# Edge sums over 32 nodes on four column groups, in batches of two chunks, and the edge half of the MLP's first layer done tile by tile among them

## Chip, cores and metric

The kernel runs on one core of one Trainium2 chip. The metric is the device time of one launch in microseconds; before the change it is 714.82 us, the median of 3 runs (714.66 to 717.14).

## What is computed

One block of a graph network. All 100,000 edges carry a row of 256 floats and a receiving node `dst`, sorted; `src` is not used in the arithmetic. There are 6,250 nodes, and the receivers are drawn as 6250 u^2, so low nodes have many edges (some 20 each around node 1,000) and high ones few (8 each at the end).

```python
aggr = jax.ops.segment_sum(edge_attr, dst, num_segments=6250)      # 102.4 MB of edges read once
collected = jnp.concatenate([layernorm(x), aggr], axis=-1)          # [6250, 512]
h = relu(collected @ W1 + b1); h = relu(h @ W2 + b2)                # 512->256->256
x = x + h @ W3 + b3
# then, on layernorm(x): slice attention with 8 heads x 64 slices
slice_weights = softmax((x_mid @ W_slice + b_slice) / temp)         # [6250, 8, 64]
# slice tokens, their attention, and the projection of slice_weights back to 256 columns, added to x
```

Everything is fp32.

## The kernel before

Three stages follow each other. The **edge stage** (to about 290 us) reads the edges in 98 chunks of 1,024 edges (1 MB) into a ring of four slots. Each chunk is eight subtiles of 128 edges. For a chunk VectorE builds one-hot matrices (`one_hot`, L752 to L757) that say for each edge which of WINDOW = 64 consecutive nodes it belongs to, counted from the lowest node of its group; TensorE multiplies them with the edge rows (`window_sums`, L1111 to L1128), which gives 64 nodes x 256 columns per group. Chunks 0 to 83 hold two groups of 512 edges, the others four groups of 256. Two groups run side by side in the array: 64 columns of weights each, and the results on the lower and the upper 64 partitions of one PSUM bank (`side_of`, L1118). ScalarE copies them to SBUF (`evacuate`, L635), TensorE turns them (`turn`, L1130), and VectorE adds each group's window into the table `agg` in SBUF at a column read from a register (L835 to L840); each add waits for the one before by `groups_added`. SyncE issues the edge loads (`chunk`, L377): a slot is loaded again once `win_psum` says that its sums are done. How a chunk's edges lie in a slot depends on the groups: chunks 0 to 39 are one stretch of eight edge rows (8 KB) per partition, 40 to 83 two of 4 KB, 84 on four of 2 KB.

Beside that, once per trip of four chunks, two tiles of x (128 nodes each) are loaded (L399), normalised (VectorE statistics L815 to L822, GpSimd L526 to L531, ScalarE L622), transposed (`ln_transposes`) and sent through the upper half of W1 (`first_layer_x`), so that `h1x` holds layernorm(x) @ W1a + b1 at the end of the stage.

The **MLP** (290 to 420 us) goes over tiles of 512 nodes, twelve full ones and a rest of 106: `layer1` multiplies `agg` by the lower half W1b, VectorE adds `h1x` (`add_h1`, L902), ScalarE applies relu (L662), `layer2`, relu (L665), `layer3`, VectorE adds to x and takes statistics (`residual`, L911 to L923), GpSimd adds b3 and computes the scale (L546, L517 to L519). The order on PE is written out by hand (L1251 to L1280): layer2(i), layer1(i+1), layer3(i). In between lie `fold_transposes`, the products that fold W_slice into W_x (L1264) and the biases (L1271).

The **attention part** follows, from the transpose at L1286 on: 49 tiles of softmax (L1293, L1310), the slice attention, and the projection of 49 tiles (L1382). The change leaves it as it is.

If some group's edges span more nodes than the window has, a flag is set (`far_flag`) and a branch computes all sums again by an exact, slow way; otherwise the branch is skipped.

Every fp32 matmul shows as two instructions in the trace; a transpose shows as one.

## Time and profile before

| | us |
|---|---|
| median of three runs | 714.82 |
| time of the profiled execution | 716.08 |
| its span | 714.3 |
| edge stage, to the last sum | 284.85 |
| MLP, from layer1(0) to the first transpose of the attention part | 290.24 to 419.28 |
| attention part | 419.28 to 714.3 |

```profile
span 714.3 us, 12349 instructions
PE 689.7 (97%) x3510; PEld 431.3 (60%) x3510; DVE 409.5 (57%) x985; ACT 305.1 (43%) x470; POOL 238.4 (33%) x308
...
PE   7899999999999999999999989999999999799997
...
DVE  6555545545555466453444378888888888522221
...
PEclk9999999999999999999999999999999999999999
DMA  8999999999999999200000004333333333212221
GB/s 314 393 375 408 393 406 408 407 405 404 407 404 404 394 384 313 75 1 0 0 0 0 0 1 60 73 70 62 73 71 62 72 73 66 38 59 73 81 81 65
...
PE 75%; DMA 20%; DVE 2%; issue 1%; SPq 1%; ACT 0%; DVEq 0%; ACTq 0%
```

The digit lines are the span in 40 slices of 17.9 us, each digit the busy share in tenths; the edge stage is the first 16 slices, where DMA is busy, the MLP the next seven. The last line is the chain of work that ended last, by engine.

### The profile page before, as it was taken

To read this page: it belongs to the slowest core of one execution; us is meant where nothing else is said; L and a number is where in the kernel's file an instruction comes from. 1 tells how busy PE (TensorE), PEld (TensorE's weight loads), DVE (VectorE), ACT (ScalarE), POOL (GpSimd) and SP (SyncE) were. 2 spreads that over 40 slices of the span, in tenths; PEclk is the share of its full clock that TensorE was granted. 3 is DMA by queue.
4 is the path that set the end of the run, shared out by engine and by line. 5 is a ranking of instruction groups with operands and counts; after the bars stand their busy time and mean duration, and the time that the engine had idled before them with its cause. 6 is when DMAs were issued, how large, how long until landed. Compare 5 with 4: busy or idle time off the path is not lost.

```text
span 714.3 us, 12349 instructions
## 1 busy us (share of the span) xinstructions
PE 689.7 (97%) x3510; PEld 431.3 (60%) x3510; DVE 409.5 (57%) x985; ACT 305.1 (43%) x470; POOL 238.4 (33%) x308
## 2 busy tenths in 40 slices
PE   7899999999999999999999989999999999799997
PEld 3666666666666666666556654444444444588886
DVE  6555545545555466453444378888888888522221
ACT  4233343333333434312221225545545545487773
POOL 3011011011010101313323336666666666254442
PEclk9999999999999999999999999999999999999999
DMA  8999999999999999200000004333333333212221
GB/s 314 393 375 408 393 406 408 407 405 404 407 404 404 394 384 313 75 1 0 0 0 0 0 1 60 73 70 62 73 71 62 72 73 66 38 59 73 81 81 65
DMA packets 95119, 131.72 MB, mean 184 GB/s; under 512 B 56825, under 2 KB 71117, under 8 KB 89983
## 3 DMA queue, kind: packets, MB, share of 16 engines
q1 hardware_dynamic: 94287, 131.26, 53.1%
q10 hardware_dynamic: 816, 0.26, 0.2%
q8 instruction: 8, 0.13, 0.1%
q14 instruction: 8, 0.07, 0.0%
HBM read 112.26 MB, written 6.40 MB: 166 GB/s over the span
## 4 chain that ended last, share of the span: by engine, by line
PE 75%; DMA 20%; DVE 2%; issue 1%; SPq 1%; ACT 0%; DVEq 0%; ACTq 0%
DMA ring_mem<-edge_attr_in 20%; PE ps L1124 14%; PE ps L1382 12%; PE ps L1293 12%; PE ps L1310 11%; PE ps L1246 6%; PE ps L1236 6%; PE ps L1228 6%; PE ps L1182 3%; PE ps L1286 2%; PE ps L1137 1%; PE ps L1174 1%; PE ps L1348 0%; DVE ring_mem L981 0%; DVE mx L983 0%
## 5 line engine op out<-in xcount | busy, mean ns | idle before, releaser
L1124 PE MATMUL ps<-ring_mem,side 128*64 128x256 f32 x1564 | 187.8, 386 | 8.1 <-DMA ring_mem<-edge_attr_in 6.0
L1124 PEld LDWEIGHTS ps<-ring_mem,side 128*64 128x64 f32 x1564 | 113.1, 137 | 68.8 <-issue 26.5
L756 DVE TENSOR_TENSOR side<-iota_w,rel 128x512 f32<-128x512 f32 x98 | 67.0, 686 | 94.2 <-PE ps L1137 94.1
L638 ACT ACTIVATE side<-ps 128x256 f32<-128x256 f32 (+1 forms) x98 | 40.7, 415 | 145.6 <-PE ps L1124 145.5
L1293 PE MATMUL ps<-ring_mem,xn 128*128 128x512 f32 x196 | 93.3, 599 | 0.9 <-DVE ring_mem L995 0.7
L1310 PE MATMUL ps<-side,ring_mem 128*128 128x512 f32 x196 | 92.3, 593 | 1.0 <-ACT ring_mem L674 1.0
L526 POOL TENSOR_TENSOR var_e<-mv,eps 128x2 f32<-128x2 f32 (+1 forms) x25 | 4.9, 195 | 237.8 <-DVE mv L822 237.8
L839 DVE TENSOR_TENSOR big<-big,ps 128x128 f32 x223 | 63.9, 287 | 30.1 <-issue 12.1
L1382 PE MATMUL ps<-side,ring_mem 128*128 128x256 f32 x360 | 77.9, 379 | 0.0
L584 POOL TENSOR_TENSOR ring_mem<-ring_mem 128x512 f32<-128x512 f32 x49 | 67.3, 1373 | 30.7 <-DVE ring_mem L995 30.1
L1382 PEld LDWEIGHTS ps<-side,ring_mem 128*128 128x128 f32 x360 | 68.4, 190 | 9.3
L689 ACT ACTIVATE ring_mem<-ring_mem 128x512 f32<-128x512 f32 x49 | 30.9, 630 | 89.5 <-POOL ring_mem L576 89.5
L735 ACT ACTIVATE ring_mem<-big 128x1024 uint16 (+1 forms) x45 | 60.7, 1358 | 15.6 <-PE ps L1382 15.6
L1310 PEld LDWEIGHTS ps<-side,ring_mem 128*128 128x128 f32 x196 | 36.9, 190 | 47.0 <-issue 45.0
L576 POOL TENSOR_TENSOR ring_mem<-ring_mem,mx 128x512 f32<-128x512 f32 x49 | 51.0, 1042 | 35.6 <-DVE mx L983 35.4
L1064 DVE TENSOR_TENSOR ring_mem<-ps,xn 128x256 f32<-128x256 f32 x49 | 20.8, 425 | 64.2 <-PE ps L1382 64.2
L602 POOL TENSOR_TENSOR xn<-x_sb,ring_mem 128x256 f32<-128x256 f32 x49 | 35.7, 732 | 55.7 <-DVE ring_mem L1064 43.2
L682 ACT ACTIVATE side<-ring_mem 128x1024 uint16<-128x1024 uint16 x49 | 51.8, 1058 | 1.0 <-DVE ring_mem L993 0.8
L1293 PEld LDWEIGHTS ps<-ring_mem,xn 128*128 128x128 f32 x196 | 33.4, 190 | 28.5 <-issue 26.0
L1182 PE MATMUL ps<-ln_t,w1a_sb 128*128 128x256 f32 (+1 forms) x200 | 48.9, 387 | 0.7 <-ACT ln_t L627 0.7
L1236 PE MATMUL ps<-ring_mem 128*128 128x512 f32 (+1 forms) x104 | 44.3, 569 | 0.8 <-ACT ring_mem L662 0.8
L1246 PE MATMUL ps<-ring_mem 128*128 128x256 f32 x196 | 44.5, 380 | 0.5 <-ACT ring_mem L665 0.5
(131 smaller groups left out, 820.1 us busy)
## 6 DMA issues: line engine op xcount, KB each, us to landing
ring_mem<-edge_attr_in SPq DMA_DIRECT2D x97, 1024.0 KB, 8.6
x_sb<-x_in SPq DMA_DIRECT2D x24, 256.0 KB, 7.0
result<-ring_mem SPq DMA_DIRECT2D x24, 256.0 KB, 2.1
big<-side SPq DMA_TRANSPOSE x49, 3.0
ring_mem<-edge_attr_in SPq DMA_DIRECT2D x1, 512.0 KB, 5.9
ring_mem<-L_gnn_W_in SPq DMA_DIRECT2D x2, 256.0 KB, 3.3
ring_mem<-L_ffn_W_x_in SPq DMA_DIRECT2D x2, 256.0 KB, 4.7
ring_mem<-L_ffn_W_fx_in SPq DMA_DIRECT2D x1, 512.0 KB, 3.7
```

Of the source, the lines that this page charges most:

```text
L584: pool.tensor_tensor(sw_sum, sw_sum, soft[:, (s - 1) % UNROLL, :], ALU.add).then_inc(sw_summed, 1)
L682: act.activation(halves[:, s % 2], words(soft[:, (s - 2) % UNROLL, :]), ACT.Copy).then_inc(split_ready, 1)
L735: act.activation(words(stage[:, s, :]), sw_t[:, bass.ds(t, 1)].rearrange("p t h n -> p (t h) n"), ACT.Copy).then_inc(staged, 1)
L756: dve.tensor_tensor(hot[:, b], iota_w[:, :].unsqueeze(1).broadcast_to(shape), where.unsqueeze(2).broadcast_to(shape), ALU.is_equal).then_i ...
L839: dve.tensor_tensor(win, win, pair[:, :, (g % 2) * WINDOW:(g % 2 + 1) * WINDOW], ALU.add).then_inc(groups_added, 1)
L1124: last = mm(ps[side_of * WINDOW:(side_of + 1) * WINDOW, SUM_BANKS[s % 2], pair * F:(pair + 1) * F], lhsT=hot[0:parts, s, t, :], rhs=ring8[ ...
L1182: last = mm(ps[:, bank, m * 256:m * 256 + n * P], lhsT=w1a_sb[:, k, m * P:(m + 1) * P], rhs=ln_t[:, k, 0:n * P], start=(k == 0), stop=(k = ...
L1236: last = mm(halves[m], lhsT=w2_sb[:, k, m * P:(m + 1) * P], rhs=h1_t[:, k, 0:cols], start=(k == 0), stop=(k == KF - 1))
L1246: last = mm(ps[:, 4 + a // 2, (a % 2) * F:(a % 2 + 1) * F], lhsT=h2_t[:, k, a * P:(a + 1) * P], rhs=w3_sb[:, k, :], start=(k == 0), stop=( ...
L1293: last = mm(ps[:, 4 + k, :], lhsT=xn[:, r, k * P:(k + 1) * P], rhs=soft[:, r, :], start=isinstance(t, int) and t == 3, stop=isinstance(t, ...
L1310: last = mm(ps[:, s % 2, :], lhsT=xn_t[:, s % 2, k, :], rhs=wc[:, k, :], start=(k == 0), stop=(k == KF - 1))
L1382: last = mm(ps[:, s, 0:F], lhsT=rows, rhs=m_blk[:, j, :], start=(j == 0), stop=(j == PAIRS - 1))
```

## The change

- **Groups and windows.** WINDOW is 32. A group is half as many edges: chunks 0 to 39 have two groups of 512, chunks 40 to 83 four of 256, and chunks 84 to 99 hold 896 edges on 112 partitions, four groups of 224. There are 100 chunks. Rows per partition are 4 KB for chunks 0 to 39 and 2 KB from 40 on.
- **Four column groups.** A group's sums take 32 columns of the array and 32 partitions of the result; four groups run side by side.
- **Batches.** PE, ACT and DVE go in batches of two chunks. With two groups per chunk, the four groups of a batch share one half of a bank, so that evacuation and turn are half as large; with four, each chunk's sums take one half. Window adds become 64 elements wide (two halves of 32) instead of 128; there are 319 instead of 223. `turn` uses two banks instead of four; banks 6 and 7 are for the new product.
- **x work.** Two tiles of x per batch instead of per trip, done by batch 27.
- **First layer for edges.** From trip 14 on, each trip of four chunks computes agg @ W1b for one tile of 512 nodes, one half per batch (`first_layer_edges`), and DVE adds it into `h1x` (`add_h1e`). Ahead of the first half PE waits until the adds of all earlier batches are done. Groups from there on take their window from no lower than the nodes already used. Eleven tiles are done so; tile 11 and the rest come after the stage.
- **MLP.** relu of the first layer reads `h1x` directly; layer2 uses two pairs of banks in turn; the order is layer2(i), layer3(i-1).
- **Loads.** W1b and W2 during the edge stage, W3 after chunk 97, b3 and W_x after the last sums, W_fx after the last third layer.

The diff, cut to its core:

```diff
-WINDOW = 64
+WINDOW = 32
+CHUNK_GROUPS = 4
 ROWS_PER_PART = 2
...
-TURN_BANKS = (2, 3, 6, 7)
+TURN_BANKS = (2, 3)
+H1E_BANKS = (6, 7)
...
+TWOS = 40
+FOURS = 84
+LAST_P = 112
+X_TRIPS = 13
+H1E_TRIP = 14
+H1E_TILES = 11
...
+def run_batches(eng, step):
+
+    def trip(i, groups, parts, what):
+        for h in range(2):
+            step(i * 2 + h, h, i, groups, parts, what)
+
+    trip(0, 2, P, "x")
+    trip(1, 2, P, "x")
+    with eng.Fori(2, TWOS // UNROLL) as i:
+        trip(i, 2, P, "x")
+    with eng.Fori(TWOS // UNROLL, X_TRIPS - 1) as i:
+        trip(i, 4, P, "x")
+    trip(X_TRIPS - 1, 4, P, "x")
+    trip(X_TRIPS, 4, P, "x")
+    with eng.Fori(H1E_TRIP, FOURS // UNROLL) as i:
+        trip(i, 4, P, "h1")
+    with eng.Fori(FOURS // UNROLL, H1E_TRIP + H1E_TILES - 1) as i:
+        trip(i, 4, LAST_P, "h1")
+    trip(H1E_TRIP + H1E_TILES - 1, 4, LAST_P, "h1")
 
 
...
+            def chunk_rows(c, groups, parts):
+                if parts == P:
+                    rows = edges[bass.ds(c * CHUNK_EDGES, CHUNK_EDGES), :]
+                else:
+                    rows = edges[bass.ds(c * LAST_EDGES + (E_LAST - FOURS * LAST_EDGES), LAST_EDGES), :]
+                return rows.rearrange("(g p k) f -> p g (k f)", g=groups, p=parts)
+
+            def slot(s, groups, parts):
+                return ring8[0:parts, s].rearrange("p (g k) f -> p g (k f)", g=groups)
...
+            def batch(b, h, i, groups, parts, what):
+                for j in range(2):
+                    c, s = b * 2 + j, h * 2 + j
+                    if past(c, UNROLL):
+                        sp.wait_ge(win_psum, c - (UNROLL - 1))
+                    if before(c, FULL_CHUNKS):
+                        sp.dma_start(slot(s, groups, parts), chunk_rows(c, groups, parts)).then_inc(edge_in[s], 16)
+                    else:
+                        tail_chunk(s, edge_in[s])
+                    if isinstance(c, int) and c == 0:
+                        rest_of_dst()
+                if isinstance(b, int) and b == 1:
...
+                if what == "x" and before(b, X_PAIRS):
+                    if past(b, 1):
+                        sp.wait_ge(x_in, b * 16)
+                    sp.dma_start(tiles_of(b * 2, 2),
+                                 x[bass.ds(b * (2 * P), 2 * P), :].rearrange("(t p) f -> p t f", p=P)
                                  ).then_inc(x_in, 16)
-
-            run_chunks(sp, chunk, 1, EDGE_TRIPS, CHUNKS, apart=True)
-
...
+                if isinstance(b, int) and b == X_PAIRS + 2:
+                    sp.dma_start(w1b_sb, w1[F:2 * F, :].rearrange("(k p) n -> p k n", p=P)).then_inc(w1b_in, 16)
+                    sp.dma_start(w2_sb, w2.rearrange("(k p) n -> p k n", p=P)).then_inc(w2_in, 16)
+            run_batches(sp, batch)
+            sp.wait_ge(win_psum, CHUNKS - 2)
+            sp.dma_start(w3_sb, w3.rearrange("(k p) n -> p k n", p=P)).then_inc(w3_in, 16)
+            sp.wait_ge(win_psum, CHUNKS)
+            sp.dma_start(b3_bc, b3.rearrange("(a n) -> a n", a=1).broadcast_to([P, F])).then_inc(b3_in, 16)
...
+            sp.wait_ge(l3_psum, MLP_CHUNKS + 1)
+            sp.dma_start(wfx_sb, w_fx.rearrange("(k p) n -> p k n", p=P)).then_inc(late_in, 16)
...
+            def relu_one(i, cols):
+                act.wait_ge(h1e_added, i * 2 + 3)
+                if past(i, 1):
+                    act.wait_ge(l2_psum, i)
+                act.activation(h1_t[:, :, 0:cols], h1x[:, :, bass.ds(i * 4 * P, cols)], ACT.Relu).then_inc(h1_ready, 1)
+
...
+            def relu_two(i, cols, halves):
                 act.wait_ge(l2_psum, i + 1)
+                if past(i, 1):
+                    act.wait_ge(l3_psum, i)
                 for m in range(KF):
                     act.activation(h2_t[:, m, 0:cols], halves[m], ACT.Relu,
                                    bias=b2_sb[:, m:m + 1]).then_inc(h2_ready, 1)
 
-            with act.Fori(0, MLP_CHUNKS) as i:
-                relus(i, 4 * P, [ps[:, 2 + m, :] for m in range(KF)])
...
+            relu_one(0, 4 * P)
+            for i in range(3):
+                relu_one(i + 1, 4 * P)
+                relu_two(i, 4 * P, l2_banks(i % 2))
...
+            with act.Fori(0, (MLP_CHUNKS - 4) // 2) as j:
+                for a in (1, 0):
+                    i = j * 2 + (4 - a)
+                    relu_one(i + 1, 4 * P)
+                    relu_two(i, 4 * P, l2_banks(a))
...
+                late = rel[:, TWOS:CHUNKS, :]
+                dve.wait_ge(prep_v, then(dve.tensor_scalar(below, late, 0.0, 8192.0, ALU.is_lt, ALU.mult)))
+                dve.wait_ge(prep_v, then(dve.tensor_tensor(late, late, below, ALU.add)))
...
+            def add_h1e(i, m, n=4, bank=None):
+                at = ps[:, H1E_BANKS[m], 0:n * P] if bank is None else ps[:, bank + m, 0:n * P]
+                cols = h1x[:, m, bass.ds(i * 4 * P, n * P)]
+                dve.wait_ge(h1e_psum, i * 2 + (m + 1))
+                dve.tensor_tensor(cols, cols, at, ALU.add).then_inc(h1e_added, 1)
...
+            def batch(b, h, i, groups, parts, what):
+                if before(b, BATCHES - 2):
+                    dve.wait_ge(win_psum, b * 2 + 2)
+                    for j in range(2):
+                        one_hot(b * 2 + (UNROLL + j), h * 2 + j)
+                if what == "h1":
+                    if h == 0:
+                        dve.wait_ge(h1x_ready, 2 * (X_PAIRS + 1))
+                    add_h1e(i - H1E_TRIP, h)
+                if h == 0:
+                    n_regs = UNROLL * groups
+                    dve.load(base_regs[0:n_regs], base_i[0:1, bass.ds(sums_ahead(b * 2, groups), n_regs)])
+                dve.wait_ge(sums_ready, b + 1)
+                turned_sums = ps[:, TURN_BANKS[h], :]
+                for j in range(2):
+                    c = b * 2 + j
+                    for g in range(groups if before(c, FULL_CHUNKS) else TAIL_GROUPS):
+                        dve.wait_ge(groups_added, sums_ahead(c, groups) + (CREDIT + g))
+                        win = agg[:, :, bass.ds(base_of[(h * 2 + j) * groups + g], WINDOW)]
+                        col, q = (0, j * 2 + g) if groups == 2 else (j * F, g)
+                        found = turned_sums[:, col:col + F].rearrange("p (k n) -> p k n", k=KF)
+                        dve.tensor_tensor(win, win, found[:, :, q * WINDOW:(q + 1) * WINDOW],
+                                          ALU.add).then_inc(groups_added, 1)
+                if what == "x" and before(b, X_PAIRS):
+                    dve.wait_ge(x_in, b * 16 + 16)
+                    for a in range(2):
+                        norm_stats(b, a)
+                    if past(b, 1):
+                        dve.wait_ge(rstd1_ready, b)
+                    norm_sums(b, 2)
...
+            for m in range(KF):
+                add_h1e(MLP_CHUNKS - 1, m)
+            for m in range(KF):
+                add_h1e(MLP_CHUNKS, m, n=1, bank=4)
...
+            def one_sum(b, h, j, g, t, q, col, parts, first, last):
+                return mm(ps[q * WINDOW:(q + 1) * WINDOW, SUM_BANKS[h], col:col + F],
+                          lhsT=hot[0:parts, h * 2 + j, t, :], rhs=ring8[0:parts, h * 2 + j, t, :], start=first, stop=last)
+
+            def window_sums(b, h, i, groups, parts):
+                pe.wait_ge(hot_ready, b * 2 + 2)
+                pe.wait_ge(edge_in[h * 2], i * 16 + 16)
+                if groups == 2:
+                    pe.wait_ge(edge_in[h * 2 + 1], i * 16 + 16)
+                    for n in range(per):
+                        for q in range(4):
+                            last = one_sum(b, h, q // 2, q % 2, (q % 2) * per + n, q, 0, parts, n == 0, n == per - 1)
+                    last.then_inc(win_psum, 2)
+                    return
+                for j in range(2):
+                    tail = not before(b * 2 + j, FULL_CHUNKS)
+                    if j == 1:
+                        pe.wait_ge(edge_in[h * 2 + 1], i * 16 + (32 if tail else 16))
+                    for n in range(per):
+                        for g in range(TAIL_GROUPS if tail else groups):
+                            rows = TAIL_PARTS if tail and g == TAIL_WHOLE else parts
+                            last = one_sum(b, h, j, g, g * per + n, g, j * F, rows, n == 0, n == per - 1)
+                    last.then_inc(win_psum, 1)
+
+            def turn(b, h, groups):
+                pe.wait_ge(win_ready, b + 1)
+                if past(b, 2):
+                    pe.wait_ge(groups_added, sums_ahead(b * 2 - 2, groups) + CREDIT)
+                for n in range(groups // 2 * KF):
+                    last = tr(ps[:, TURN_BANKS[h], n * P:(n + 1) * P], win_sb[:, h, n * P:(n + 1) * P], ident[:, :])
+            def first_layer_edges(i, m, n=4, bank=None):
+                to = ps[:, H1E_BANKS[m], 0:n * P] if bank is None else ps[:, bank + m, 0:n * P]
+                for k in range(KF):
+                    last = mm(to, lhsT=w1b_sb[:, k, m * P:(m + 1) * P], rhs=agg[:, k, bass.ds(i * 4 * P, n * P)],
+                              start=(k == 0), stop=(k == KF - 1))
+                return last
+
+            def batch(b, h, i, groups, parts, what):
+                window_sums(b, h, i, groups, parts)
+                if what == "x":
+                    if past(b, 3):
+                        first_layer_x(b - 3, 1 if isinstance(b, int) and b == X_PAIRS + 3 else 2)
+                    if past(b, 2) and before(b, X_PAIRS + 3):
+                        ln_transposes(b - 2, 1 if isinstance(b, int) and b == X_PAIRS + 2 else 2)
+                else:
+
+                    if h == 0:
+                        pe.wait_ge(w1b_in, 16)
+                        pe.wait_ge(h1x_ready, 2 * (X_PAIRS + 1))
+                        pe.wait_ge(groups_added, sums_ahead(b * 2, groups) + CREDIT)
+                    pe.wait_ge(h1e_added, (i - H1E_TRIP) * 2 + 1)
+                    first_layer_edges(i - H1E_TRIP, h).then_inc(h1e_psum, 1)
+                turn(b, h, groups)
...
+            pe.wait_ge(w2_in, 16)
+            pe.wait_ge(groups_added, sums_ahead(CHUNKS - 2, CHUNK_GROUPS) + CREDIT)
+            layer2(0, 4 * P, l2_banks(0))
+            pe.wait_ge(groups_added, CREDIT + ALL_SUMS)
+            pe.wait_ge(h1e_added, 2 * H1E_TILES + 1)
             for m in range(KF):
+                first_layer_edges(MLP_CHUNKS - 1, m).then_inc(h1e_psum, 1)
+            for m in range(KF):
+                first_layer_edges(MLP_CHUNKS, m, n=1, bank=4).then_inc(h1e_psum, 1)
+            layer2(1, 4 * P, l2_banks(1))
+            pe.wait_ge(w3_in, 16)
+            pe.wait_ge(h1e_added, 2 * (MLP_CHUNKS + 1) + 1)
             layer3(0, 4)
+            fold_transposes()
+            layer2(2, 4 * P, l2_banks(0))
             layer3(1, 4)
+            fold_weights()
+            layer2(3, 4 * P, l2_banks(1))
+            layer3(2, 4)
+            fold_biases()
+            with pe.Fori(0, (MLP_CHUNKS - 4) // 2) as j:
+                for a in (0, 1):
+                    i = j * 2 + (4 + a)
+                    layer2(i, 4 * P, l2_banks(a))
+                    layer3(i - 1, 4)
+            layer2(MLP_CHUNKS, P, [ps[:, 1, m * P:(m + 1) * P] for m in range(KF)])
             layer3(MLP_CHUNKS - 1, 4)
```

## Rows read from the trace of the kernel before

**Rows 1.** Busy time in stretches of the edge stage and of the MLP, PE to GB/s
```profile
0.00:20.00 20.00, 14.53 (x81) 7.83 (x81) 13.93 (x31) 9.25 (x5) 5.69 (x16) 1.00 0.85 313
60.00:120.00 60.00, 59.46 (x464) 40.34 (x466) 30.14 (x92) 22.77 (x51) 6.17 (x20) 1.00 1.01 403
180.00:240.00 60.00, 59.10 (x466) 40.09 (x464) 30.46 (x91) 22.63 (x50) 6.17 (x20) 1.00 1.03 405
246.00:270.00 24.00, 22.98 (x180) 16.08 (x178) 14.31 (x46) 9.80 (x18) 2.58 (x7) 1.00 1.05 384
303.00:415.00 112.00, 112.00 (x364) 67.27 (x362) 50.47 (x135) 24.78 (x33) 35.68 (x32) 1.00 0.00 0
```

**Rows 2.** Chain of waits in the edge stage; columns: start, length, what, instructions
```profile
231.71 8.74 DMA ring_mem<-edge_attr_in
254.31 10.53 DMA ring_mem<-edge_attr_in
269.71 3.60 PE ps L1124 x32
```

**Rows 3.** Timeline, edge stage, PE; columns: start, length, engine, line, what, idle before
```profile
182.46 0.66 PE L1174 MATMUL ps<-ident,xn 128*128 128x128 f32 x4
182.95 0.60 PE L1137 MATMUL ps<-ident,side 128*128 128x128 f32 x4
187.49 1.99 PE L1182 MATMUL ps<-ln_t,w1a_sb 128*128 128x256 f32 x8
259.55 1.95 PE L1124 MATMUL ps<-ring_mem,side 128*64 128x256 f32 x16 [0.75 <-DMA ring_mem<-edge_attr_in]
```

**Rows 4.** Groups of instructions; columns as in the page's part 5
```profile
L1124 PE MATMUL ps<-ring_mem,side 128*64 128x256 f32 x1564 | 187.8, 386 | 8.1 <-DMA ring_mem<-edge_attr_in 6.0
L1124 PEld LDWEIGHTS ps<-ring_mem,side 128*64 128x64 f32 x1564 | 113.1, 137 | 68.8 <-issue 26.5
L839 DVE TENSOR_TENSOR big<-big,ps 128x128 f32 x223 | 63.9, 287 | 30.1 <-issue 12.1
L981 DVE TENSOR_TENSOR ring_mem<-ps,side 128x512 f32<-128x512 f32 x49 | 33.9, 691 | 18.4 <-PE ps L1310 17.7
```

**Rows 5.** Timeline of DVE in the edge stage
```profile
185.30 0.43 DVE L815 BATCH_NORM_STATS2 bn<-x_sb 128x6 f32 x1
276.11 1.55 DVE L839 TENSOR_TENSOR big<-big,ps 128x128 f32 x4 [1.02 <-issue]
```

**Rows 6.** Timeline at the end of the edge stage, and line L388's landing
```profile
273.78 0.47 SPq L388 DMA_DIRECT2D ring_mem<-edge_attr_in  x1
...
DMA to landing us min/median/max: 7.3/7.3/7.3
...
281.18 3.67 PE L1124 MATMUL ps<-ring_mem,side 128*64 128x256 f32 x28
290.24 3.60 PE L1228 MATMUL ps<-big,side 128*128 128x512 f32 x8
```

**Rows 7.** Chain of waits in the MLP, one tile, then timeline at its end
```profile
342.12 3.43 PE ps L1228 x8
345.56 3.45 PE ps L1246 x16
349.01 3.43 PE ps L1236 x8
...
419.28 0.38 PE L1286 MATMUL ps<-ident,xn 128*128 128x128 f32 x2
```

**Rows 8.** Timeline of DVE, ACT and POOL beside one tile of the MLP
```profile
380.22 1.22 DVE L911 TENSOR_TENSOR x_sb<-x_sb,ps 128x1024 f32 x1 [2.29 <-PE ps L1246]
381.55 1.41 DVE L916 BATCH_NORM_STATS2 bn<-x_sb 128x6 f32 x4
383.44 1.27 ACT L665 ACTIVATE ring_mem<-ps,b_sb 128x512 f32<-128x512 f32 x2 [4.42 <-PE ps L1236]
384.86 2.35 POOL L546 TENSOR_TENSOR x_sb<-x_sb,ring_mem 128x1024 f32 x1
```

602 lines of the change are left out of this document (251 added, 351 removed).

## The prediction

> **What bounds the kernel now.** I read the stretches first. From 60 to 240 us, while edges are summed, the DMA engines are saturated at 403 to 405 GB/s, and PE is busy 59 of 60 us: two engines at their limit at once. From 246 on, where a chunk is stored in 2 KB rows instead of 4 KB, the rate is 384. From 303 to 415 no DMA runs and PE is busy all the time [rows 1]. The chain of waits says the same: it goes through landings of 8.74 us, and of 10.53 us where the rows are 2 KB [rows 2]. PE waits for the landing there, too (0.75 us at 259.55) [rows 3], so 384 is DMA's rate, not PE's. The MLP is one unbroken line of PE: three layers of 3.43 to 3.45 us per tile of 512 nodes [rows 7]. So a cut of PE's work in the edge stage alone gives nothing, as DMA stays; PE time made free there is worth something only if MLP work is moved into it. That is the change.
>
> **Sums on four column groups.** A chunk is 16 PE instructions (each fp32 matmul is two); two chunks together take 3.60 us [rows 2], 0.225 us per pair of instructions that run side by side on two column groups (one lasts 386 ns, 1564 of them fill 187.8 us [rows 4]). With four groups side by side the 32 instructions of a batch take 8 x 0.225 = 1.8 us; I take 2.0. Bounds: 1.8, and 3.6 if four are no better than two. The Trainium skill, TensorE: Matmul & The Clock Gate, Part 3, measured 2.38x for three column groups; that efficiency gives an estimate of 2.15 us, which hides as well.
> PE per batch in the x phase: 2.0 + 0.66 (four transposes of x) + 1.99 (first layer of x) + 0.3 (turn: two instructions for two chunks instead of four; 0.6 and four instead of eight where a chunk has four groups) [rows 3] = 5.0 us. DMA needs for it (1024 KB a chunk, 256 KB of x, by the page's list of issues) 2 x 1.049 MB + 0.262 MB of x at 405 GB/s = 5.82 us. DVE: two one-hots of 256 elements, each 0.42 (an operation takes 287 ns on 128 elements and 691 on 512, so 1.05 ns per element [rows 4]), four adds of 0.35 (below), 1.25 of x statistics (0.43 twice and three small steps [rows 5]), 0.3 of register loads: 4.0 us. DMA stays the bound, PE's cut is hidden, worth 0.
>
> **DMA of the edge stage.** Chunks 0 to 39 go from 8 KB rows (403) to 4 KB (405) [rows 1]: 0. Chunks 40 to 83 go from 4 KB to 2 KB: 44 x 1.049 MB x (1/384 - 1/405) = +6.2 us. Bound below: 0. By the Trainium skill, DMA: Bandwidth & Descriptors, Why small descriptors are slow, a packet carries about 3 fixed cycles beside one per 32 bytes; an estimate from that is 2.3%, 2.6 us instead of 6.2. I stay with the row.
> The w1b and w2 loads come into the stage: 0.52 MB at 384, +1.4. Before, the last chunk was issued at 273.78 and landed 7.3 us later, 281.1 [rows 6]; now 281.1 + 6.2 + 1.4 = 288.7. Batches release two slots at once; two others, 5.2 us of transfers, are then still queued, so DMA doesn't starve while sums end within that. At the start DVE gets two operations more on the index table (480 elements, some 0.65 each), PE waits for them ahead of the flag's transpose, and the next batch of sums is queued behind; the same queue of transfers covers it: 0, bound 3 us either way. The index table itself is one DMA more on SP, 0.4 us, ahead of the second chunk: in the same bound.
> Chunks 84 to 99 use 112 partitions. No row shows such a transfer. I take the rate of 384 (4 x 0.917 MB, 9.56 us per four chunks); the other end is that such a chunk takes as long as one on 128 partitions, 10.9 per four. That end speaks against the change, and the Trainium skill has a rule for it, SBUF — State Buffer, Door 1: a port serves eight partitions from separate stretches, and partitions 112 to 127 share their four ports with 80 to 95; a transfer without them leaves the other twelve ports as full as before, so by that rule 10.9.
>
> **First layer for edges inside the stage.** Each of 11 trips (four chunks) gets 3.44 us of PE [rows 7] and two DVE adds of 512 elements, 0.69 each [rows 4]. Sums, half a layer, turn: 2.0 + 1.72 + 0.6 = 4.3 us per batch against 4.8 to 5.46 of DMA. But there is a new wait: in each even batch PE waits until the previous batch's window adds are done; behind it stand its layer half, its turn and the next sums. DVE's adds also double in number (8 per batch). An add costs 0.42 from start to start (four in 1.55 [rows 5]), 0.13 of that beyond its 287 ns; at 64 elements 220 + 130 = 0.35, eight 2.8 us. 16 registers for the addresses cost 1.02 us [rows 5]. The loop per trip: PE half layer to its landing in DVE 2.1, add 0.69, registers 1.02, adds 2.8, two one-hots 0.83, add 0.69, adds 2.8 = 10.9 us. DMA wants 10.92 for the seven trips on 128 partitions (hidden) and 9.56 for the last four: +1.35 x 4 = +5.4 us. Bounds: 0 if DVE's steps overlap better, and if an add stays at 0.42, 12.0 us per trip: 7 x 1.1 + 4 x 2.45 = +17.4. Last sums end at 288.7 + 5.4 + 0.9 (one short chunk) = 295.0, where they end at 284.85 now [rows 6]: **+10.1**.
>
> **Tail and MLP.** Now 134.4 us pass from the end of the sums (284.85) to 419.28, where the attention part's first transpose starts [rows 6, 7]. Afterwards, in a row on PE: half layer 1.72, turn 0.55, twelve second layers 41.2, the small second layer 1.0 (moved ahead of that point), layer one of tile 11 and of the rest 4.4, twelve third layers 41.4, eight fold transposes 1.0, 24 instructions of fold products 3.1 (those on 128 columns at 0.13, from 0.60 for four [rows 3] less the drain): 94.4 us. **-40.0**. Eleven x 3.43 = 37.7 of it is the moved layer, the rest the x layer and transposes that stand now between 284.85 and 290.24 [rows 6]. Beside a tile of 6.9 us lie DVE 1.22 + 1.41 + 0.7 of small steps, ACT 1.27 and one more relu of that size, POOL 2.35 and some 1.4 of small steps [rows 8]: each under 4 us, their cover holds, and without it POOL would be next. The first second layer (3.43) covers the last seven window adds (2.5). The small second layer left its place after 419.28 (1.0), but DVE's last residual (3.4 us) ends last there: -0.2. The w_fx load waits for the last third layer, SP's transposes stand behind it; it costs 3.7 us of queue at most, with four tiles to go before a buffer comes back: 0. The w3, b3 and w_x loads land some 10 us before PE wants them: 0.
>
> **Sum**: +10.1 - 40.0 - 0.2 = -30.1. Profiled span 714.3 gives 684.2; that run's time was 716.08, 1.78 around the span; it lay 1.26 above the median 714.82. That gives **684.7**.
>
> **Rivals.**
> (a) The hand-over chain is longer: an add stays at 0.42 for the smaller window. For: the 0.13 between adds is waiting, not elements. Against: 512 and 128 elements do scale. 684.7 + 12 = 696.7. Chance 0.17.
> (b) DMA is kinder: 2 KB rows at 405 once PE is free, and DVE hides. Then 281.1 + 1.4 + 0.9 = 283.4: 684.7 - 11.6 = 673.1. Against: 384 held in a stretch where PE waited for DMA. 0.10.
> (c) Four groups no better than two: sums 3.6 per batch. x phase 6.6 against 5.82 in 20 batches and 6.8 against 6.14 in four: +17.5; edge trips 11.9 against 10.9: +11. 713. 0.06, no measurable change.
> (d) Slower than before: the weight loads of the narrow tiles don't overlap one another. A load lasts 137 ns, though now only 72 of it count (113.1 / 1564) [rows 4]. 32 x 0.137 = 4.4 us per batch: x phase 7.4 against 5.8 (+31 + 6 + 3), edge trips 13.5 against 10.9 (+28): 753. It decides from 3.7 us per batch, where the gain is gone. 0.05.
> (e) PE now idles 1 us or so in each batch, and the granted clock falls to 1.2 GHz: 4.3 becomes 8.6, 5.0 becomes 10, some +175 us. Against: it stayed at 1.00, that is 2.4 GHz, in the first 20 us too, with PE busy 14.5 of them [rows 1]. The Trainium skill, TensorE: Matmul & The Clock Gate, Part 1, has idleness bring the half clock back. 0.02.
> (f) It doesn't do what it says: if a group of edges spans over 32 nodes, the exact fallback branch runs as well, for milliseconds. The sorted indices that the reference draws span at most 30 nodes in a group (of 512, 256 or 224 edges). 0.01.
> Forecast: 0.59.
>
> **Range and chances.** The forecast's own range, with 3 us of start and the DMA bounds, is 674 to 692. Down to (b) and up to (a) with the same start: 671 to 700, 0.86 of the chance. A measurement tells about 0.5% (3.6 us) from no change: faster under 711.2: 0.87; same 0.05; slower 0.08.
>
> **What would show it.** Right: about 405 GB/s until chunk 40, 384 after, PE busy under 90% in the stage; a batch of sums in 2.0 us; last sums near 295; MLP tiles of 6.9 us with PE without gaps; from the last sums to the first attention transpose about 94 us; that part itself unchanged. Wrong: a batch of sums over 2.9 us (PE bound), PE idle ahead of the edge half-layer by over 2 us per trip (chain), a granted clock under 1.00, or a tile over 7.5 us, which would mean that POOL or ACT took PE's place.

## The result, and the profile after

The changed kernel takes 710.57 us (median of 7 runs, 707.6 to 719.46); the kernel before took 715.48 in the same session. The ratio is 0.9925, with a 95% interval of 0.9897 to 0.9954: a gain of 0.5 to 1.0%. The forecast was 684.7 us, in a range of 671 to 700. The direction was right, five sixths of the gain didn't come.

The profiled execution of after is its slow one, 719.46 us (span 717.7), 8.9 above the median; the ratio above leaves it out, the ledgers below are made on its span, and where the other executions are shorter isn't seen in it.

Busy time by stretches, core 0 of after; columns as in [rows 1]: PE, PEld, DVE, ACT, POOL, then granted clock, DMA share (how busy the core's 16 DMA engines were on average), GB/s:
```profile
60.00:120.00 60.00, 46.56 (x469) 34.04 (x468) 28.17 (x115) 28.40 (x61) 15.13 (x44) 1.00 1.03 402
120.00:180.00 60.00, 47.54 (x481) 31.68 (x483) 30.66 (x127) 28.39 (x58) 11.62 (x32) 1.00 1.05 384
180.00:240.00 60.00, 47.36 (x434) 21.28 (x427) 33.67 (x120) 6.57 (x11) 0.00 (x0) 1.00 1.05 387
245.00:320.00 75.00, 52.29 (x353) 22.46 (x355) 29.05 (x102) 4.78 (x8) 0.00 (x0) 0.78 1.08 218
```
Up to 240 us this is the forecast: 402 GB/s with 4 KB rows, 384 to 387 with 2 KB rows, PE at 79% where it was at 99% [rows 1]. From 245 on the DMA engines are as busy as ever (1.08), and move little more than half as much. What is in flight there stands in the list of DMA issues of the page (engine, operation, count, KB each, median us to landing):
```profile
ring_mem<-edge_attr_in SPq DMA_DIRECT2D x84, 1024.0 KB, 8.8
ring_mem<-edge_attr_in SPq DMA_DIRECT2D x15, 896.0 KB, 15.9
```
The second kind is the chunks on 112 partitions, 84 to 98, called the late chunks below. The chain of waits goes through them, in pieces of 15 to 17 us; one of the four (start, length, what):
```profile
266.24 16.77 DMA ring_mem<-edge_attr_in
```
Before, the longest pieces of that kind were 8.74 and 10.53 [rows 2]. Four such chunks, one trip, now take about 18 us; the forecast had 10.9.

PE's timeline shows a batch of sums in the x phase (the batches that also work on tiles of x, up to 182 us), two half layers (one half of `first_layer_edges` of a tile, L1232) beside full-width transfers, the end of the sums, and the end of the MLP:
```profile
63.19 1.93 PE L1197 MATMUL ps<-ring_mem,side 128*32 128x256 f32 x32 [1.06 <-DMA ring_mem<-edge_attr_in]
...
194.84 1.98 PE L1232 MATMUL ps<-big,side 128*128 x4 [0.22 <-DVE big L924]
...
239.05 1.98 PE L1232 MATMUL ps<-big,side 128*128 x4 [1.06 <-DVE big L924]
...
325.24 3.14 PE L1197 MATMUL ps<-ring_mem,side 112*32 112x256 f32 x28
328.31 1.98 PE L1232 MATMUL ps<-big,side 128*128 128x512 f32 x4
...
419.39 3.69 PE L1328 MATMUL ps<-ring_mem 128*128 128x256 f32 x16 [0.70 <-DVE x_sb L998]
423.59 0.44 PE L1390 MATMUL ps<-ident,xn 128*128 128x128 f32 x2 [0.51 <-DVE xn L1048]
```
32 instructions on four column groups take 1.93 us; 16 on two took as long [rows 3]. The next two follow 6.06 and 5.86 us behind, and PE waits for the landing in each. In the edge trips PE waits for the window adds ahead of the half layer, 0.22 us at 194.84 and 0.2 more in each trip, 1.06 at 239.05: the hand-over chain is 11.05 us per trip and slowly falls behind the transfers, which need 10.84. VectorE's side of one trip, with the half layers that it serves at 216.96 and 221.65 and the next one at 228.00 (L897 adds a half layer into `h1x`, L924 the windows, L813 makes the masks):
```profile
219.11 0.69 DVE L897 TENSOR_TENSOR big<-big,ps 128x512 f32 x1 [1.34 <-PE ps L1232]
221.05 2.70 DVE L924 TENSOR_TENSOR big<-big,ps 128x64 f32 x8 [1.25 <-issue]
223.78 0.76 DVE L813 TENSOR_TENSOR side<-iota_w,rel 128x256 f32<-128x256 f32 x2
224.45 0.68 DVE L897 TENSOR_TENSOR big<-big,ps 128x512 f32 x1
225.05 2.68 DVE L924 TENSOR_TENSOR big<-big,ps 128x64 f32 x8
```
The 1.25 us that the view charges to nothing is where VectorE loads 16 registers; the register edit below bears that out.

The sums end at 328.38 (284.85 before [rows 6]), and the attention part starts at 423.59 (419.28 before [rows 7]). An MLP tile, three lines of the chain of waits before [rows 7], is two now, 6.88 us, with no gap:
```profile
366.14 3.45 PE ps L1328 x16
369.59 3.43 PE ps L1318 x8
```

The ledger against the forecast: last sums 328.38 instead of 295.0, +33.4; from there to the attention part 95.2 instead of 94.4, +0.8; attention part to the end 294.1 instead of 294.8, -0.7. Sum +33.5, as 717.7 stands to 684.2. All of it lies in the edge stage. The forecast's own terms put the landing of chunk 83 at 288.7 - 15 x 2.39 - 1.4 = 251.4 (fifteen late chunks and the short last one come behind it), and the end of its sums 2.0 later, at 253.4; it was 255.9 (the half layer behind it starts at 255.93). So 2.5 us came before the 112-partition chunks and 30.9 with them: those 16 chunks took 72.5 us, 14.3 MB at 198 GB/s. The median execution is 8.9 us shorter and so misses the forecast by 25.9; if all of the 8.9 lies in these chunks, which isn't shown, they took 63.6 us there (an estimate, 225 GB/s), and 22.0 of its 25.9 us are theirs.

### The profile page after: what moved, and what is told of

The parts are those of the page before. It is cut to its first block, busy times and chain, and to the rows that moved or that the text cites. A ratio compares the mean times of both kernels' runs of the same rounds, so it can differ in the third digit from the quotient of the medians.

```text
span 717.7 us, 12605 instructions
## 1 busy us (share of the span) xinstructions
PE 625.6 (87%) x3481; PEld 367.6 (51%) x3481; DVE 397.8 (55%) x1103; ACT 287.5 (40%) x422; POOL 242.1 (34%) x310
## 4 chain that ended last, share of the span: by engine, by line
PE 53%; DMA 41%; DVE 3%; issue 1%; SPq 1%; POOL 0%; DVEq 0%; POOLq 0%
DMA ring_mem<-edge_attr_in 21%; DMA x_sb<-x_in 20%; PE ps L1485 12%; PE ps L1397 12%; PE ps L1414 11%; PE ps L1318 6%; PE ps L1328 5%; PE ps L1197 3%; PE ps L1390 2%; PE ps L1232 1%; PE ps L1451 0%; DVE bn L1003 0%; DVE x_sb L998 0%; DVE ring_mem L1065 0%; SPq L425 0%
## 5 line engine op out<-in xcount | busy, mean ns | idle before, releaser
L1197 PE MATMUL ps<-ring_mem,side 128*32 128x256 f32 (+1 forms) x1596 | 113.8, 413 | 69.9 <-DMA ring_mem<-edge_attr_in 69.7
L924 DVE TENSOR_TENSOR big<-big,ps 128x64 f32 x319 | 70.7, 221 | 93.6 <-PE ps L1226 43.8
L1197 PEld LDWEIGHTS ps<-ring_mem,side 128*32 128x32 f32 (+1 forms) x1596 | 50.5, 115 | 116.0 <-DMA ring_mem<-edge_attr_in 54.0
L675 ACT ACTIVATE side<-ps 128x512 f32<-128x512 f32 (+1 forms) x50 | 25.6, 512 | 205.9 <-PE ps L1197 205.9
L744 ACT ACTIVATE ring_mem<-ring_mem 128x512 f32<-128x512 f32 x49 | 30.9, 630 | 90.3 <-POOL ring_mem L610 90.3
L1232 PE MATMUL ps<-big,side 128*128 (+2 forms) x104 | 60.1, 714 | 4.5 <-DVE big L924 4.5
L813 DVE TENSOR_TENSOR side<-iota_w,rel 128x256 f32<-128x256 f32 x100 | 37.9, 421 | 33.7 <-PE ps L1197 31.9
L1397 PEld LDWEIGHTS ps<-ring_mem,xn 128*128 128x128 f32 x196 | 33.4, 190 | 28.5 <-issue 25.9
```

Source lines behind the costliest of these rows:

```text
L924: dve.tensor_tensor(win, win, found[:, :, q * WINDOW:(q + 1) * WINDOW], ALU.add).then_inc(groups_added, 1)
L1197: return mm(ps[q * WINDOW:(q + 1) * WINDOW, SUM_BANKS[h], col:col + F], lhsT=hot[0:parts, h * 2 + j, t, :], rhs=ring8[0:parts, h * 2 + j, ...
L1232: last = mm(to, lhsT=w1b_sb[:, k, m * P:(m + 1) * P], rhs=agg[:, k, bass.ds(i * 4 * P, n * P)], start=(k == 0), stop=(k == KF - 1))
L1397: last = mm(ps[:, 4 + k, :], lhsT=xn[:, r, k * P:(k + 1) * P], rhs=soft[:, r, :], start=isinstance(t, int) and t == 3, stop=isinstance(t, ...
```

## The experiments

Two theories came first. A: a transfer to 112 partitions is slow by itself, whatever the kernel does beside it. B: the hand-over chain of PE and VectorE (rival a), or the granted clock, which is 0.78 from 245 to 320, holds the late trips, and the transfers only wait for buffers. The expectations add a C: the late chunks' place in memory is slow.

**All partitions.** The last chunks are loaded on all 128 partitions: the 16 partitions more read rows that another group of the same chunk holds, and nobody uses them.
```
+            def wide_rows(c, groups, parts):
+                a = chunk_rows(c, groups, parts)
+                return bass.AP(a.tensor, a.offset, [[a.ap[0][0], P]] + [list(d) for d in a.ap[1:]])
...
-  sp.dma_start(slot(s, groups, parts), chunk_rows(c, groups, parts)).then_inc(edge_in[s], 16)
+  sp.dma_start(slot(s, groups, P), wide_rows(c, groups, parts)).then_inc(edge_in[s], 16)
```


> The changed kernel, but chunks 84 to 98 are loaded on all 128 partitions: each group of 224 edges takes 32 rows of the next group with it, and the sums still read 112 partitions only. Bytes of these chunks rise by 1/7, all else stays. Theory A (a transfer on 112 partitions is slow in itself): these chunks run at 384 to 388 GB/s as the ones before them, 10.8 to 11 us per four chunks instead of about 18, the last sums end near 295 instead of 328, and the median falls by 26 to 31 us, to 680 to 685. Theory B (the hand-over between PE and VectorE, with PE at half clock, starves the ring from chunk 84 on): no gain or a few us of loss, 708 to 716. Theory C (what is slow is the smaller chunk's place in memory, groups of 224 rows): the same places are read, so no gain either.

Measured: 695.29 us, ratio to before 0.973 (0.970 to 0.977). The stretch with the late chunks in this kernel, columns as above:
```profile
245.00:298.00 53.00, 41.75 (x388) 19.93 (x380) 29.91 (x107) 5.97 (x10) 0.00 (x0) 0.97 0.99 354
```
More bytes are moved in less time: 354 GB/s instead of 218, and the sums end at 303.52. Against the kernel before, the gain grows from 4.9 to 19.9 us, so 15 us come back for one changed access pattern. Theories B and C, which had no gain, are out, and theory A holds as to the cause. Its size was missed: it had 680 to 685 us, the sums done near 295 and trips of 10.8 to 11 us. The trips took 11.05 us up to 227.90 and 11.0 to 13.1 after; the last sections come back to that.

**Transfers by themselves.** No sums and no MLP are computed here, the result is a copy of x; only rows are loaded, four transfers in flight, eight of each kind. One kind of eleven:
```
...
+  for c in range(8):
+      free(c % 4)
+      got(sp.dma_start(slot(c % 4, 112, 4, 512), rows(c + 8, 112, 4, 512)), c % 4)
+  end()
...
```


> Only loads, no sums: this leaves the whole computation out and copies x to the result. Eight transfers each, four slots in flight, of edge rows in pieces of 2 KB to 128, 112, 96, 64 and 120 partitions, then 112 partitions in pieces of 4 KB and 8 KB, 112 split into 64 and 48, 112 partitions' groups of 224 rows read on 128 partitions, and 128 partitions in pieces of 4 KB and 8 KB. Theory A: 112 gives some 200 GB/s here too, 128 some 385 (2 KB) and 400 or more (4 and 8 KB), and the wide read of 224-row groups 385. If A's cause is that the engines then meet at the same ports, 96 and 120 are slow as well and 64 too (half the ports). Theory B: 112 gives 370 or more. Theory C: 112 in groups of 224 is slow, and so is the wide read of the same groups.

Stretches of this kernel, within each set; no engine but DMA works, so clock, DMA share and GB/s count. In order: 128, 112, 96, 64 and 120 partitions with 2 KB rows; then 112-partition chunks loaded on 128; then 128 partitions with 8 KB rows:
```profile
5.00:23.00 18.00, 0.00 (x0) 1.00 1.05 390
30.00:50.00 20.00, 0.00 (x0) 1.00 1.06 297
57.00:77.00 20.00, 0.00 (x0) 1.00 1.06 242
85.00:100.00 15.00, 0.00 (x0) 1.00 1.07 212
108.00:140.00 32.00, 0.00 (x0) 1.00 1.00 205
...
245.00:263.00 18.00, 0.00 (x0) 1.00 1.04 389
...
291.00:308.00 17.00, 0.00 (x0) 1.00 1.01 425
```
For 112 partitions, 297 GB/s is neither theory A's 200 nor theory B's 370: slow by themselves, but not as slow as in the kernel. Only full width reaches 390, and the rate isn't a share of the partitions: 120 of them give 205, less than 112 or 96. Longer rows don't help 112 partitions (304 with 4 KB, 283 with 8 KB), though they help 128 (413, 425); 64 + 48 in two transfers gave 190.

The Trainium skill, SBUF — State Buffer, Door 1, has bandwidth follow from how many of 16 ports the partitions reach. The forecast read it so that the fullest ports set the time: 112 partitions would take as long as 128, seven eighths of 390, 341 GB/s (an estimate). 297 misses that, 205 for 120 partitions misses it by far, and only 64 partitions (212, where the page has half of the ports) agree.

**Two transfers per chunk.** The kernel after, with each late chunk as 64 + 48 partitions.
```
+  sp.dma_start(to[0:64], a[0:64]).then_inc(edge_in[s], 16)
+  sp.dma_start(to[64:parts], a[64:parts]).then_inc(edge_in[s], 16)
```


> The changed kernel, but each load of chunks 84 to 98 is two transfers, one on partitions 0 to 63 and one on 64 to 111. If 112 partitions are slow because 7 per engine lay the engines across each other, while 4 and 3 per engine don't, these chunks reach 350 or more and the time falls to about 685 to 690. If the number of ports that are in use at one time decides, the first piece keeps the engines to half of them: 200 GB/s again, 705 to 712. Theory B: no change, about 710.

Measured in a single execution: 718.32 us, and 221 GB/s from 245 to 320 where after has 218. Splitting is no cure; the blocks of 4 and 3 partitions per engine that the expectation counted on didn't reach 350.

**Where the 200 GB/s comes from.** Alone 112 partitions gave 297, in the profiled execution of after 198. Three kernels take up the difference. The first two load rows and compute nothing of the reference. The first puts the transfers at other spacings and behind full-width ones.
```
+  stream(24, 112, 1024, 0)
+  stream(24, 112, 896, 25088)
+  stream(8, 128, 1024, 50176)
+  stream(16, 112, 896, 60416)
```

> Transfers alone, 2 KB rows, four in flight, the MLP and the edge sums left out (the result is a copy of x), in four stretches: 24 transfers on 112 partitions that start 1024 edge rows apart; 24 on 112 partitions in one piece of memory (896 rows apart); 8 on 128 partitions and straight behind them 16 on 112; 24 on 128. The kernel after ran its 112-partition transfers at about 200 GB/s, an isolated set of eight ran at 299. If a lasting stream is what slows them, the first three stretches fall to about 200 after some eight transfers (918 KB each in 4.6 us). If the position in memory does, the first stays at 299 and the second and third fall to 200. If a start right behind full-width transfers does, only the third falls. If none, all stay at 299, and the slow rate of the kernel comes from what the engines do beside it. The last stretch gives 385 to 400 in every case.

It gave 270, 271 and 297 GB/s in the three stretches on 112 partitions, and 387 on 128. None fell to 200, but the first two weren't at 299 either: the same count gives 270 to 303 in different stretches, with no engine at work, and no run says why. The second takes the kernel's own addresses (arguments: count, partitions, spacing, first row), and lets engines work beside the transfers.
```
+  stream(15, 112, 896, 86016)
+  stream(15, 112, 896, 32768)
+  stream(15, 120, 1024, 8192)
+  stream(15, 128, 896, 86016)
```

> Transfers alone (MLP and edge sums left out, the result is a copy of x), 15 at a time, four in flight, 2 KB rows, with a pause between stretches. In order: 112 partitions at exactly the edge rows of the kernel's last chunks (from 86016); 112 partitions from row 32768, where an earlier sweep had 120 partitions at 205 GB/s; 120 partitions from row 8192, where that sweep had 112 at 299; 128 partitions from row 86016; then the first stretch again with TensorE multiplying beside it, and again with VectorE adding beside it. If the partition count sets the rate, 112 gives 260 to 300 and 120 about 205 wherever they lie, and 128 gives 385. If the place in memory does, the first stretch gives about 200, the second about 205, the third about 299. If the engines' work beside it does, the first stretch gives 260 to 300 and the fifth or sixth about 200. The kernel had 200 GB/s.

Stretches of this kernel, one in each set; PE, PEld, DVE, POOL busy, then clock, DMA share, GB/s:
```profile
4.00:44.00 40.00, 0.00 (x0) 0.00 (x0) 0.00 (x0) 0.00 (x0) 1.00 1.06 302
52.00:90.00 38.00, 0.00 (x0) 0.00 (x0) 0.00 (x0) 0.00 (x0) 1.00 1.06 303
104.00:160.00 56.00, 0.00 (x0) 0.00 (x0) 0.00 (x0) 0.00 (x0) 1.00 1.00 208
178.00:212.00 34.00, 0.00 (x0) 0.00 (x0) 0.00 (x0) 0.00 (x0) 1.00 1.05 388
222.00:258.00 36.00, 34.68 (x642) 20.59 (x631) 0.00 (x0) 0.00 (x0) 1.00 1.06 262
272.00:304.00 32.00, 31.09 (x572) 17.54 (x560) 30.50 (x45) 0.00 (x0) 1.00 1.06 266
```
The place in memory does nothing here: 302 at the kernel's own rows, 303 elsewhere, 208 for 120 partitions where the sweep had 205 at other rows. With PE working beside, the same rows gave 262; VectorE beside it takes nothing more (266; in this stretch PE still worked too, so VectorE alone wasn't seen). That PE's work takes the 40 GB/s is a reading, not shown: the stretches of the kernel just above lay at 270 without any engine, and PE reads another buffer here, not the ring. The third is the kernel after with almost all of PE's sums of the late chunks gone:
```
+  if parts == LAST_P and not tail:
+      for g in range(groups):
+          last = mm(ps[g * WINDOW:(g + 1) * WINDOW, SUM_BANKS[h], j * F:j * F + 32],
+                    lhsT=hot[0:parts, h * 2 + j, g * per, :],
+                    rhs=ring8[0:parts, h * 2 + j, g * per, 0:32], start=True, stop=True)
```


> The kernel after, unchanged in its transfers (112 partitions for the last chunks), but the sums of those chunks are cut to one product of 32 columns per group: most of their edges and columns are left out of the result. TensorE's 1.93 us per batch become a few tenths, VectorE's masks and adds stay, so the hand-over chain of such a trip falls below 8 us. If the engines' reading of the ring beside the transfers is what holds them at 200 GB/s (alone they ran at 260 to 304, beside 1800 products or 100 adds at 230 to 260), the late trips fall from 18 us to 12 to 14 and the rate rises to 260 to 300: about 690 to 697 us. If the transfers' own split is, the trips stay at 17 to 18.5 us and about 200 GB/s, and the time stays within 2 us of the kernel after.

Measured in a single execution: 714.54 us, 241 GB/s from 265 to 310 where the profiled execution of after has 203 from 265 to 320, trips of 14.3 to 15.4 us, sums done at 320.2 instead of 328.4. Neither expectation came. That PE's reading of the ring costs part of the rate isn't shown by it: 714.54 us is no gain over after's median of 710.57, and the trace it is held against is of after's longest execution. What it shows is that even nearly without that reading the trips are far from 10.9. Why these transfers run at 198 to 241 GB/s in the kernel and at 270 to 303 alone stays open.

**Why the partition count matters.** In the sweep the DMA share for 120 partitions was 1.00, not 1.05 to 1.07: as if 15 of 16 engines worked. One more kernel, with loads on other counts, tests that share.
```
...
+  stream(12, 126, 1024, 12288)
+  stream(12, 104, 1024, 24576)
+  stream(12, 100, 1024, 36864)
+  ...
```


> Loads alone (MLP and sums left out, the result is a copy of x), 2 KB rows, four in flight, on 128, 126, 104, 100, 80, 124 and 127 partitions in this order. So far 128 gave 390 GB/s at a DMA share of 1.05, 120 gave 205 to 208 at a share of 1.00, 112 gave 297 to 303, 96 gave 242 and 64 gave 212 at 1.06 to 1.07. Theory C: the partitions are dealt to the DMA engines in equal blocks, and only as many engines work as divide the count: 14 for 126, 13 for 104, 10 for 100, 16 for 80, 4 for 124, 1 for 127. Then the DMA share of a stretch is that number of sixteenths of 1.06 (0.93, 0.86, 0.66, 1.06, 0.26, 0.07), and no rate is over the engines' number times 24.4 GB/s (390 / 16): at most 341, 317, 244, 390, 98 and 24; where blocks meet at the same ports it is less, about half for 104 as for 120. This is the Trainium skill's rule in DMA: Bandwidth & Descriptors, How many engines. Theory D: the 16 engines share every transfer evenly, and the rate falls off with the partitions left out by the fullest port or by count: then the share is 1.05 in every stretch, 124, 126 and 127 give 340 to 390, 104 and 100 give 250 to 300, and 80 gives 200 to 250.

Stretches, one in each set of 128, 126, 104, 100, 80, 124 and 127 partitions; clock, DMA share, GB/s:
```profile
5.00:28.00 23.00, 0.00 (x0) 1.00 1.05 389
38.00:70.00 32.00, 0.00 (x0) 1.00 0.91 346
88.00:128.00 40.00, 0.00 (x0) 1.00 0.87 189
145.00:175.00 30.00, 0.00 (x0) 1.00 0.66 222
190.00:213.00 23.00, 0.00 (x0) 1.00 1.07 234
235.00:265.00 30.00, 0.00 (x0) 1.00 0.26 101
282.00:312.00 30.00, 0.00 (x0) 1.00 0.07 26
```
The shares are those of this expectation's theory C to within 0.02, down to 124 partitions on four engines and 127 on one; three rates lie a little above its caps (346, 101 and 26 where it had 341, 98 and 24). Theory D is out. So a transfer works on as many engines as the largest number up to 16 that divides its partition count. For 112 that is all 16, seven partitions each, and its share is full; its loss must be a second thing. The rate per working engine is 24.3 GB/s for 128 (389 / 16), 24.7 for 126, 22.2 for 100, 25 for 124 and 26 for 127, but 18.6 for 112 (297 / 16), 15.1 for 96, 14.6 for 80, 14.5 for 104, 13.7 for 120 and 13.3 for 64. Every count with fewer than nine partitions per engine loses, but for the 128 itself.

The Trainium skill offers a reason for these. By SBUF — State Buffer, Door 1, partitions come in fours, p and p + 32 lie at one port, and 0 to 63 reach eight of the sixteen ports. By DMA: Bandwidth & Descriptors, The descriptor swizzle, a transfer to 128 partitions gives each engine a port of its own. If the other counts are dealt in plain blocks, 64 partitions put two engines on each of eight ports, and with blocks of eight (120, 104) engines e and e + 4 go through the same two ports in step, so both would get about half a rate, which fits the 13.3 to 14.5; blocks of seven (112) meet only part of the time, blocks of nine (126) never in step. It doesn't fit all: by the same working blocks of ten (100) meet more often than blocks of seven, and are faster. So this part of the mechanism is argued, not shown: no run here sees a port.

**Does the chain or DMA set the edge trips?** As the first experiment, but from trip 14 on (half layers, from 182 us) only two of four groups are loaded; the sums of the others run on old data, so a part of the edges is left out.
```
+  if what == "h1":
+      to, a = to[:, 0:2], a[:, 0:2]
```


> As the wide loads, but from trip 14 on only the first two of the four groups of each chunk are loaded (the sums of the other two take what lies in the slot: part of the edges is left out), so that DMA needs 5.4 us per four chunks. What is left is the hand-over between PE and VectorE. My sum for it was 10.9 us per trip of four chunks; if the steps overlap better, 8.6 to 10 us, with PE's own work (2 x 4.3) as the floor. If an add of 64 elements costs as much as one of 128, 12. The last sums end at 150 + 11 times that.

Measured in a single execution: 694.35 us; from 185 to 225 DMA moves 184 GB/s at a share of 0.53. PE's half layers in this kernel:
```profile
205.20 1.98 PE L1239 MATMUL ps<-big,side 128*128 x4 [1.79 <-DVE big L931]
...
216.25 1.98 PE L1239 MATMUL ps<-big,side 128*128 x4 [2.56 <-DVE big L931]
```
Half the bytes, and the trip stays at 11.05 us: the hand-over chain sets it, as the forecast's 10.9 had it, and neither 8.6 to 10 nor 12. (The expectation's end of the sums, 150 plus eleven trips, began the count 30 us too early: they ended at 300.5.)

**Shorten the chain.** The first experiment's kernel, with VectorE's loading of 16 registers moved ahead of its wait for the half layer.
```
-add_h1e(i - H1E_TRIP, h)
 if h == 0:
     n_regs = UNROLL * groups
...
+if what == "h1":
+    add_h1e(i - H1E_TRIP, h)
```


> As x1_wide128, but VectorE loads the registers of the next x batch before, not behind, the eight adds of an h1 trip, so that they overlap TensorE's half layer. If the hand-over chain of TensorE and VectorE sets the trip (11.05 us in x1_wide128 with 1.1 us of register loading in it), the trip falls to about 10.0 by the chain, and the transfers become the bound at 10.7 to 10.9 us: 1 to 2 us less over the whole, 693 to 694.5 us. If transfers set the trips already, nothing changes: 695 us, trips of 11.05.

Measured: 691.3 us (690.41 to 691.95), ratio 0.967 (0.965 to 0.969), 4.0 less than with the first edit alone, more than the 1 to 2 expected, and the lowest median of this study. PE's half layers and a stretch of it:
```profile
206.54 1.98 PE L1237 MATMUL ps<-big,side 128*128 x4 [0.22 <-DVE big L929]
...
217.37 1.98 PE L1237 MATMUL ps<-big,side 128*128 x4 [0.21 <-DVE big L929]
...
245.00:295.00 50.00, 40.72 (x363) 18.38 (x362) 27.83 (x99) 5.38 (x9) 0.00 (x0) 1.00 1.04 376
```
Trips are 10.83 us (one is 11.11), the wait no longer grows, and DMA is the bound; sums are done at 300.7. The clock is 1.00 in this stretch where it was 0.97 without the edit, so part of the 4.0 may be the clock's. The forecast needs little correction for this kernel: the 15 x 0.131 MB that the wider loads move more cost 5.1 us at 387 GB/s, but the 5.4 us that it had for the chain in the late trips go, as four chunks now take 10.8 us by DMA anyway. That gives 294.7 for the last sums and 684.4 for the time, against 300.7 and 691.3: with the slow transfers cured, 6 to 7 us are missing still. Some 1.6 of them are there by chunk 83, and 1.4 lie in the last sums, which take 2.27 us behind the last landing where 0.9 was put; the rest isn't broken down.

**The granted clock.** In the first experiment's kernel some instructions ran near 1.2 GHz (a half layer in 3.64 us instead of 1.98, at a granted clock of 0.89 from 220 to 230), and a trip with one was longer, 12.70 us here:
```profile
227.90 3.64 PE L1236 MATMUL ps<-big,side 128*128 x4 [1.49 <-DVE big L928]
...
240.60 2.90 PE L1236 MATMUL ps<-big,side 128*128 x4 [2.55 <-DVE big L928]
```
Two kernels add matmuls on unread data where PE waits: the first is that kernel plus these, the second has the register edit too.
```
+                        keep_busy(1, 4, 5)
+                    if h == 1:
+                        keep_busy(1, 2, 5)
+                if what == "x" and past(b, 4):
+                    keep_busy(1, 2, 7)
```


> As x1_wide128 (last chunks on all 128 partitions), with matmuls on data that nobody reads put ahead of TensorE's wait for the adds of each trip (20), behind the half layer (10) and behind each x batch from the fifth on (14). x1_wide128's trips took 11.05 us up to 227.90 and then 12.70, 11.98, 11.04, 11.27 and 13.13 us, with the granted clock at 0.91 over 240 to 280, and its half layer at 3.64 instead of 1.98 us in the dipped trips. If the dips are what the trace charges to them, the clock stays at 1.00, the late trips come back to about 11.05 to 11.3 us, and the time falls by 5 to 8 us, to 687 to 690 us. Rival: the fillers stand in the chain and the late trips are long for another reason (transfers): then the time is 695 us or above, with late trips still over 11.8 us at a clock of 1.00.

> x5_fill's and x6_regs's edits together. If both theories hold: 686 to 688.5 us, trips of 10.7 to 10.9 us with the clock at 1.00 to the last sums, which end at about 294 to 297 us of the span. If only the clock matters: 687 to 690. If neither: 695.

Measured: 699.8 us for the first (698.41 to 701.32), 694.29 for the second (690.32 to 700.29). Both expectations failed: the medians are 4.5 and 3.0 us above the same kernels without the filler. In the first the clock was 1.00 from 60 to 300 and the sums ended at 300.5, 3.0 us earlier, so the dips are worth about that. But right behind the sums stands this:
```profile
307.48 6.59 PE L1327 MATMUL ps<-ring_mem,side 128*128 128x512 f32 x8 [4.15 <-issue]
...
305.00:310.00 5.00, 2.52 (x3) 1.17 (x4) 0.54 (x3) 0.00 (x0) 4.42 (x2) 0.65 0.12 20
```
PE stood 4.15 us for nothing that the trace names, and the clock was at 0.65 afterwards; those layers took 6.59 us instead of 3.60. From the last sums to the attention part 102.9 us passed instead of 95.2. Why PE stood there wasn't settled. The profiled execution of the second kernel, 690.92 us, has as long a program and no such pause: its second layer starts at 303.24, right behind the turn at 302.81. The six executions of that kernel fall into two lots, 690.3 to 691.5 and 697.1 to 700.3; that the pause is what parts them is a guess, as only one was traced. Even the lower lot is no faster than the kernel without the filler (691.3), where the clock was up already.

## Why the prediction was wrong, step by step

- **What bounds the kernel**: right. DMA at 402 and 384 to 387 GB/s, with PE waiting for it in the x phase.
- **Four column groups**: right. 1.93 us for a batch (2.0 forecast, 1.8 to 3.6 as bounds). Batches of the x phase start 5.9 to 6.1 us apart, DMA's term was 5.82. Rivals (c), four groups no better than two, and (d), serial weight loads, are out with this row.
- **DMA of chunks 0 to 83**: nearly right. 2 KB rows cost 44 x 1.049 MB x (1/386 - 1/402) = 4.8 us (6.2 forecast). The 2.6 us estimated from the Trainium skill, DMA: Bandwidth & Descriptors, Why small descriptors are slow, were too few. The sums of chunk 83 ended 2.5 us late, in the bound of 3. Most of that is the start: over the first 60 us DMA moved 350 GB/s where it had moved 366, which at 402 is 2.3 us; the forecast put 0 there.
- **Chunks 84 to 99**: this step failed. "No row shows such a transfer. I take the rate of 384", with 10.9 us per four chunks as its other end. The bound was made from the full-width transfer, as if leaving partitions out could at worst gain nothing. It made the transfer slower: 18 us per four chunks in the kernel, 198 GB/s, and 270 to 303 GB/s with nothing beside it. The same chunks on 128 partitions took 10.83. The step was worth 30.9 of the 33.4 us of the profiled execution, and the range, which had no case for it, missed. The port rule was read as the pessimistic end, but the page counts the ports reached, and not how engines are dealt to them; the 10.9 drawn from it was six tenths of the price.
- **Hand-over chain**: right in kind and size, 11.05 us for 10.9. By its parts: half layer to landing 2.15 (2.1), adds of the half layer 0.69 and 0.68 (0.69), registers 1.25 (1.02), eight window adds 2.70 and 2.69 (2.8), masks 0.76 (0.83). Rival (a), 12.0 us, is out: an add on 64 elements starts every 0.34 us. Hidden behind 18 us of transfer it cost nothing in after; with that taken away it cost, as the register edit shows, up to 4 us, perhaps part of it by the clock.
- **Tail and MLP**: right, 95.2 us for 94.4. PE's waits for the last residual (0.70) and for VectorE's xn (0.51), for which the sum had no term on this side of its mark, are more than the 0.8. Of the forecast 40.0 us, 39.2 did leave this stretch.
- **Clock (rival e)**: dips came, to 0.78 in the late stage of after, and were worth about 3 us where DMA wasn't in the way. It wasn't the +175 us of the rival, nor nothing. The forecast's sign "a granted clock under 1.00" came, and pointed the wrong way: in after PE waits for landings in these trips.
- **Slips in the working**: the lower end of the range is 673.1 - 3 = 670, not 671, and rival (c)'s x phase comes to +18.2, not +17.5. Neither changes a conclusion.

So of the 30.1 us of the forecast, the change as it stands brings 4.9, with the late loads on all partitions 19.9, and with the register edit too 24.0 (715.3 to 691.3). That the direction was right is luck in part: 39.2 us left the MLP, but in the profiled executions the edge stage grew by 43.5, and there after is 3.4 us slower than before (717.7 against 714.3); only the medians have it 4.9 faster.

## What to carry to other kernels

A transfer on other than 128 partitions is another kind of transfer: price it from a measurement of that count, and if there is none, put half the rate in the range; loading all 128 partitions with unused rows can be the cheaper way. For a count with no large divisor up to 16 even half was far too much (101 GB/s for 124, 26 for 127). Read DMA share and GB/s together: a full share at half the GB/s says that the transfers are slow, a low share that engines have no work or that few of them take part (0.26 with four transfers always in flight to 124 partitions).

Once work has been moved off the busiest engine, write the hand-over loop down operation by operation: here its sum was right to 1.5%, and it named the 1.25 us that could be taken out by moving one block of lines.
